# Eight-layer network on two interleaved streams: wait steps folded into instruction steps, and new turn tables

## The chip, the cores and the metric

One NeuronCore of one Trainium2 chip runs the whole program. The metric is device time in microseconds (us) of one execution; several executions are timed and their median is quoted. The profile is of one further execution, taken by the hardware profiler.

## The reference

Four sequences of 512 tokens by 128 features pass through eight residual layers, all in float32. Each is `x = x + layer(layernorm(x))`:

```python
x = x + L0_attn(ln(x))   # 0: state-space scan, 16 heads, conv of width 4, gate, layer norm, projection
x = x + L0_ffn(ln(x))    # 1: token-shift mix, sigmoid gate, squared relu
x = x + L1_attn(ln(x))   # 2: Mamba block, inner width 256, 16 states, softplus, exp, scan
x = x + L1_ffn(ln(x))    # 3: top-2 of 8 experts, gelu
x = x + L2_attn(ln(x))   # 4: causal linear attention, 16 heads
x = x + L2_ffn(ln(x))    # 5: ternary weights, silu, two gelu layers
x = x + L3_attn(ln(x))   # 6: gated selective scan, RMS norm
x = x + L3_ffn(ln(x))    # 7: top-2 of 8 experts, silu gate
```

## The kernel before

The four sequences are played as two streams, here called stream a (sequences 0 and 2) and stream b (1 and 3). A stream runs its layers one after the other for its first sequence, then for its second; layers 3 and 7 (the experts) may take both sequences of a stream at once (`PLAYS`). Stream a takes layers 0 to 6 twice and then layer 7 for both; stream b takes layers 0 to 2 twice, then layer 3 for both, then layers 4 to 6 twice, then layer 7. Below, "b 7" is stream b in layer 7, and a second pass is called so. Each stream has its own four PSUM banks and its own working tiles, so that one stream's work can fill the other's waits.

Every engine runs one instruction list, in which the two streams are interleaved by hand-made tables. On each engine a layer is a Python generator; each `yield` ends a *turn*. `RUNS[engine]` lists run lengths: so many turns of stream a, so many of stream b, and so on. `walk` takes them in that order, so the tables are the instruction order. A turn is no instruction: it holds zero or more waits on semaphores and the instructions behind them. An engine takes its list in order, so a wait of one stream holds back all that stands behind it, of the other stream too. SyncE issues nearly all loads and stores (`SP_MOE`, `SP_ALONE` give the order inside an expert layer); the expert weights go through a ring of 4 slots, and the load of block q waits until block q-4's result has been added (L627, after the DVE instruction of L1421).

Names used later. In layer 2: `m_scan` waits at L1338 and L1340, the scans at L1341, and ScalarE's silu of the convolved rows at L882, the eight-row copy L885, softplus L890 to L895, the decays `exp` L908. In the experts: TensorE up L1829 (layer 3) and L1858 (layer 7 and the down products), ScalarE's gelu L957 and silu L954, DVE's product L1459 and result L1421, the gathers of results by GpSimd L727, and the weighted sum L1432. Layer 5: ScalarE's silu L984. Layer 6: `exp` at L1006 and from L1017 on. SyncE: expert weights L629, slots in L637, results out L641, final output L647.

In some places a wait has a turn to itself, or a turn is empty: in the Mamba layer on TensorE (L1755) and on DVE (L1337), in `turn_block` (L1662), before the scores (L1699), in layers 1 and 5 of TensorE.

## Time and profile before

| | us |
|---|---|
| median of 3 runs | 1415.96 |
| lowest, highest run | 1413.04, 1419.31 |
| span of the profiled execution | 1400.6 |
| TensorE busy | 1104.8 (79%) |
| DVE (VectorE) busy | 890.9 (64%) |
| ScalarE (ACT) busy | 630.4 (45%) |
| GpSimd (POOL) busy | 281.7 (20%) |

The profile gives the time from the first to the last instruction (the span), busy time of each engine, TensorE's granted clock as a share of full speed, the chain of work that ended last, and each instruction with what released it. The median of the timed runs is 15.4 us above the span; the profile's own time beyond its span is not given apart.

### The profile page before, as it was taken

The page shows a single profiled execution, that of the slowest core. Times are in us where ns is not written, and L with a number is a line of the kernel's source. Part 1 is how long each engine was busy: PE and PEld are TensorE (multiplying, and loading weights), DVE is VectorE, ACT ScalarE, POOL GpSimd, SP SyncE. Part 2 cuts the span into 40 slices and gives each one's busy share as a digit, 9 for nine tenths or more (in the row PEclk, how much of TensorE's full clock was granted, in tenths as well). Part 3 has the DMA queues.
Part 4 walks back from the last instruction along what each step waited for, and adds up shares of the span by engine and source line. Part 5 has one row for each costly group of instructions (what it writes and reads, how often), then busy time and mean ns, then how long its engine had stood idle before and what let it go on. Part 6 is the DMA issues. An engine that isn't in the chain of part 4 may idle for free.

```text
span 1400.6 us, 15057 instructions
## 1 busy us (share of the span) xinstructions
PE 1104.8 (79%) x4959; PEld 698.7 (50%) x4959; DVE 890.9 (64%) x1919; ACT 630.4 (45%) x1194; POOL 281.7 (20%) x258
## 2 busy tenths in 40 slices
PE   4978657767977979686768676799999899897791
PEld 2536312334743634353457442574555556787781
DVE  6787879987558767767635789723735652363432
ACT  3433385424552348634237972273252434542330
POOL 3000113324120002130230244202000032014404
PEclk9999877777989999878889897999999999899996
DMA  8100000003520000000125420370000014468782
GB/s 322 47 0 1 0 0 0 0 1 118 163 61 1 0 0 1 0 0 0 45 92 177 131 74 21 96 224 21 1 1 0 1 63 132 157 214 283 260 277 69
DMA packets 49411, 107.02 MB, mean 76 GB/s; under 512 B 4840, under 2 KB 32368, under 8 KB 48688
## 3 DMA queue, kind: packets, MB, share of 16 engines
q1 hardware_dynamic: 44656, 92.74, 20.7%
q0 software_dynamic: 4096, 8.40, 2.0%
q10 hardware_dynamic: 576, 4.87, 0.8%
q8 instruction: 41, 0.67, 0.2%
q14 instruction: 42, 0.34, 0.1%
HBM read 91.24 MB, written 14.75 MB: 76 GB/s over the span
## 4 chain that ended last, share of the span: by engine, by line
PE 41%; DVE 22%; ACT 13%; issue 9%; POOL 7%; DMA 6%; SPq 1%; DVEq 0%; POOLq 0%; ACTq 0%
PE ps L1920 6%; PE ps L1638 5%; DMA expert_ring<-in_e_dram 4%; PE ps L1586 4%; PE ps L1752 4%; DVE up L1341 3%; PE ps L1858 3%; POOL slots_dram L717 3%; ACT big L957 2%; PE ps L1692 2%; PE ps L1829 2%; PE ps L1958 2%; DVE big L1348 2%; POOL up L727 2%; PE ps L1909 1%
## 5 line engine op out<-in xcount | busy, mean ns | idle before, releaser
L1858 PE MATMUL ps<-big,expert_ring 128*128 128x128 f32 x1160 | 158.0, 286 | 33.6 <-DMA expert_ring<-in_e_dram 20.4
L1858 PEld LDWEIGHTS ps<-big,expert_ring 128*128 128x128 f32 x1160 | 145.2, 199 | 48.0 <-DMA expert_ring<-in_e_dram 26.9
L1341 DVE TENSOR_TENSOR_SCAN up<-cv,big 128x512 f32<-128x512 f32 x128 | 152.5, 1230 | 21.5 <-ACT cv L908 17.4
L660 POOL TENSOR_TENSOR rstd<-ve,nhalf 128x4 f32<-128x4 f32 (+1 forms) x41 | 47.2, 1153 | 577.2 <-DVE ve L1119 470.6
L1752 PE MATMUL ps<-big,consts 128*128 128x512 f32 x256 | 154.3, 735 | 2.4 <-DVE big L1348 2.4
L697 POOL TENSOR_TENSOR big<-big,mt 128x512 f32<-128x512 f32 x64 | 85.8, 1344 | 279.1 <-ACT mt L901 152.6
L1920 PE MATMUL ps<-big,weights 128*128 128x512 f32 x256 | 115.4, 597 | 0.0
L1769 PE MATMUL ps<-q,row_pick 96*128 96x512 bf16 x128 | 54.5, 448 | 76.6 <-DVE big L1348 61.4
L1829 PE MATMUL ps<-expert_ring,big 128*128 128x128 f32 x792 | 107.6, 280 | 5.9 <-ACT big L957 3.6
L1829 PEld LDWEIGHTS ps<-expert_ring,big 128*128 128x128 f32 x792 | 98.9, 195 | 15.3 <-ACT big L957 9.8
L1459 DVE SCALAR_TENSOR_TENSOR big<-ps,expert_ring,key 128x128 f32<-128x128 f32 x184 | 51.8, 344 | 79.6 <-PE ps L1858 67.4
L908 ACT ACTIVATE cv<-big,nega 128x512 f32<-128x512 f32 x128 | 87.2, 715 | 14.2 <-DVE up L1341 13.6
L954 ACT ACTIVATE key<-ps,expert_ring 128x128 f32<-128x128 f32 x184 | 52.6, 369 | 88.4 <-PE ps L1858 88.3
L901 ACT ACTIVATE mt<-ps 128x512 f32<-128x512 f32 x64 | 38.2, 598 | 115.4 <-PE ps L1769 110.9
L1586 PE MATMUL ps<-weights,big 128*128 128x128 f32 x608 | 79.3, 288 | 11.0 <-DVE big L1355 5.3
L1752 PEld LDWEIGHTS ps<-big,consts 128*128 128x128 f32 x256 | 59.6, 234 | 54.8 <-issue 45.5
L1586 PEld LDWEIGHTS ps<-weights,big 128*128 128x128 f32 x608 | 75.1, 201 | 21.5 <-DVE big L1355 6.9
L1890 PE MATMUL ps<-qkv_parts,selectors_rounded 128*128 128x512 f32 x192 | 72.2, 490 | 16.4 <-DVE up L1496 12.7
L1348 DVE TENSOR_TENSOR big<-up,ps 128x1024 f32<-128x1024 f32 x64 | 77.6, 1213 | 11.6 <-PE ps L1752 10.7
L717 POOL DMA_INDIRECT slots_dram<-cv,key x64 | 64.0, 1000 | 90.4 <-DVE key L1402 72.5
L1638 PE MATMUL ps<-big,mt 128*128 128x512 f32 x160 | 77.4, 643 | 4.3 <-ACT big L808 4.3
L1769 PEld LDWEIGHTS ps<-q,row_pick 96*128 96x128 bf16 x128 | 13.7, 109 | 127.3 <-DVE big L1348 83.5
(247 smaller groups left out, 1943.4 us busy)
## 6 DMA issues: line engine op xcount, KB each, us to landing
expert_ring<-in_e_dram SPq DMA_DIRECT2D x46, 836.0 KB, 5.3
expert_ring<-in_e_dram SPq DMA_DIRECT2D x53, 578.0 KB, 4.4
big<-slots_dram SPq DMA_DIRECT2D x21, 256.0 KB, 3.5
results_dram<-mt SPq DMA_DIRECT2D x21, 256.0 KB, 5.3
weights<-in_w_dram ACTq DMA_DIRECT2D x1, 3072.0 KB, 15.5
slots_dram<-big SPq DMA_DIRECT2D x2, 1024.0 KB, 10.3
weights<-in_w_dram SPq DMA_DIRECT2D x1, 1600.0 KB, 8.6
x<-in_x_dram SPq DMA_DIRECT2D x4, 256.0 KB, 13.6
```

The lines of the kernel that those rows point to most:

```text
L697: pool.tensor_tensor(BIG2[s][:, 1, :], BIG1[s][:, 3, :], MT[s][:, 0:T], ALU.mult).then_inc(m_d1[s], 1)
L717: pool.indirect_dma_start(xs_d[s % NS], bass.IndirectOffsetOnAxis(ap=posu[:, j:j + 1], axis=0), xh[h][:, c, :], None).then_inc(scattered[s ...
L908: act.activation(CV[s][:, j, :], BIG1[s][:, j, :], ACT.Exp, scale=nega[:, j * NM + n:j * NM + n + 1]).then_inc(m_da[s], 1)
L1341: dve.tensor_tensor_scan(UP[s][:, j, PAD:PAD + T], CV[s][:, j, :], BIG2[s][:, j, :], 0.0, ALU.mult, ALU.add).then_inc(m_scan[s], 1)
L1348: dve.tensor_tensor(BIG2[s][:, 2:4, :], UP[s][:, :, PAD:PAD + T], bank(s, 3).unsqueeze(1).broadcast_to([P, 2, T]), ALU.mult).then_inc(m_sc ...
L1586: last = pe.matmul(bank4(s, k)[:, c, :], lhs(b, c), rhs(b), start=(b == 0), stop=(b == blocks - 1))
L1638: last = pe.matmul(bank(s, c), MT[s][:, m:m + P], BIG2[s][:, k, :], start=(k == 0), stop=(k == c))
L1752: pe.matmul(bank(s, j), ident, BIG2[s][:, 2 + j, :], start=(n == 0), stop=(n == NM - 1))\
L1829: last = pe.matmul(bank4(s, 2 + b % 2)[:, 0, :], HID[s][:, b % 4, k * P:(k + 1) * P], wd[:, k * P:(k + 1) * P], start=(k == 0), stop=(k == 3))
L1858: last = pe.matmul(bank4(s, r if m else b % 2)[:, k, :], ring[:, q % RING, r * T + k * P:r * T + (k + 1) * P], XGT[s][:, b // 4 % 4, b % 4 ...
L1890: last = pe.matmul(bank(s, k), SELR[:, m * P:(m + 1) * P], PARTS[:, part, src, :], start=(part == 0), stop=(part == 1))
L1920: last = pe.matmul(bank(s, j), w(name, (4 * b + j) * P, P), BIG1[s][:, src + b, :], start=(b == 0), stop=(b == 3))
```

## The change

The diff has two parts. In the code, turns that hold only a wait or nothing are dropped, and their wait goes into the turn of the instruction behind it. The lists shorten: TensorE from 1237 to 1121 turns, DVE from 903 to 839; ScalarE keeps 704, GpSimd 239, SyncE 157. All five tables of run lengths are then replaced; the three long ones are left out here.

```diff
     "pool": [
-        1, 1, 1, 1, 1, 1, 1, 1, 1, 1, 2, 2, 4, 1, 2, 1, 2, 1, 2, 1, 2, 1, 2, 1, 2, 2, 1, 2, 8, 8, 9, 3, 1,
-        9, 1, 4, 1, 1, 1, 1, 1, 17, 1, 2, 14, 3, 1, 3, 1, 4, 1, 4, 1, 2, 1, 1, 9, 1, 10, 3, 1, 1, 18, 19,
+        0, 1, 1, 1, 2, 1, 1, 1, 1, 1, 2, 2, 3, 1, 1, 1, 1, 1, 2, 1, 3, 1, 2, 1, 3, 1, 1, 1, 1, 2, 8, 8, 9, 2,
+        1, 9, 1, 5, 2, 2, 1, 15, 1, 4, 13, 1, 1, 3, 1, 1, 1, 3, 1, 5, 1, 3, 1, 1, 9, 1, 10, 3, 1, 1, 18, 19,
         16, 16],
     "sp": [
-        1, 1, 23, 35, 57, 7, 1, 6, 1, 4, 1, 20],
+        2, 1, 22, 35, 56, 1, 1, 3, 1, 7, 1, 5, 1, 21],
 }
...
@@ dve, mamba @@
-                    yield
-                    dve.wait_ge(m_scan[s], m_scan.at(s, 4 * n))
                     for j in range(2):
                         yield
+                        if j == 0:
+                            dve.wait_ge(m_scan[s], m_scan.at(s, 4 * n))
                         dve.wait_ge(m_da[s], m_da.at(s, 2 * n + j))
...
@@ pe, turn_block @@
-                    yield
-                    if j >= 2:
-                        pe.wait_ge(l0_yn[s], l0_yn.at(s, j - 2))
                     for c in range(NC):
                         yield
+                        if c == 0 and j >= 2:
+                            pe.wait_ge(l0_yn[s], l0_yn.at(s, j - 2))
...
@@ pe, state_space and feed_forward @@
                     else:
-                        yield
                         pe.wait_ge(l0_key[s], l0_key.at(s, 0))
...
                 pe.wait_ge(wsem[1], 16)
-                yield
                 pe.wait_ge(f0_mix[s], f0_mix.at(s, 0))
...
@@ pe, mamba @@
-                    yield
-
-                    if n == 0:
-                        pe.wait_ge(m_mix[s], m_mix.at(s, 0))
-                        pe.wait_ge(m_sp[s], m_sp.at(s, 1))
                     for k in range(2):
                         yield
+                        if n == 0 and k == 0:
+                            pe.wait_ge(m_mix[s], m_mix.at(s, 0))
+                            pe.wait_ge(m_sp[s], m_sp.at(s, 1))
...
@@ pe, ternary @@
-                        yield
+                        if j or r:
+                            yield
...
-                    yield
-                    if src == 0:
-                        pe.wait_ge(t_h0[s], t_h0.at(s, 3))
                     for j in range(4):
                         for b in range(4):
                             yield
+                            if src == j == b == 0:
+                                pe.wait_ge(t_h0[s], t_h0.at(s, 3))
```

Laying both tables over the generators gives the order of every engine. Four stretches of it, of ScalarE and at the end of SyncE and DVE (a number behind a name is the block or the step; "up" copies, "z" silu, "s" silu, "dt" softplus, "a" exp, "b", "d8", "gt", "xT", "xs" copies; "h" product, "res" result, "gs" weighted sum):

```
ScalarE, b 3 beside a 2 (second pass)
 before  xT b:act8 up0 up1 z0 z1 s0 b:act9 s1 b:gt5 d8 b:act10 dt0 b:act11 dt1
 after   xT up0 b:act8 up1 z0 z1 s0 s1 b:act9 d8 b:gt5 b:act10 dt0 b:act11 dt1
ScalarE, a 3 beside b 5
 before  b:sa0 act8 act9 b:sa1 act10 act11 b:sa2 act12 act13 b:sa3 act14
 after   b:sa0 b:sa1 act8 act9 act10 act11 act12 b:sa2 b:sa3 act13 act14
ScalarE, a 7 beside b 6 (second pass)
 before  act3 b:ea b:xs0 act4 b:xs1 gt4 act5 b:ex act6
 after   act3 act4 b:ea b:xs0 b:xs1 b:ex gt4 act5 act6
SyncE, a 7 ends and b 7 begins
 before  w22 y4 b:w0 b:w1 b:x0 b:x1 b:x2 b:x3 b:w2 y5 b:w3 b:x4 b:w4 b:w5 b:w6 b:x5 out b:w7 b:y0 b:w8 b:w9 out b:w10
 after   w22 b:w0 y4 b:w1 b:x0 b:x1 y5 b:x2 b:x3 b:w2 b:w3 b:x4 b:w4 b:w5 out b:w6 b:x5 b:w7 b:y0 b:w8 out b:w9 b:w10
DVE, the same place (gs0.0 to gs1.1 are of stream a, h and res of stream b)
 before  h1 res0 h2 res1 gs0.0 h3 res2 h4 gs0.1 res3 h5 gs1.0 res4 h6 res5 gs1.1 h7
 after   h1 res0 gs0.0 h2 res1 h3 gs0.1 res2 h4 res3 h5 res4 gs1.0 gs1.1 h6 res5 h7
```

## Rows read from the trace of the kernel before

**Rows 1.** Page, busy time, share of the span and instructions of each engine.
```profile
PE 1104.8 (79%) x4959; PEld 698.7 (50%) x4959; DVE 890.9 (64%) x1919; ACT 630.4 (45%) x1194; POOL 281.7 (20%) x258
```
**Rows 2.** Cores view: span and mean granted TensorE clock.
```profile
core 0: 1400.6 us, clock 0.886
```
**Rows 3.** Page, chain that ended last, shares of the span.
```profile
PE 41%; DVE 22%; ACT 13%; issue 9%; POOL 7%; DMA 6%; SPq 1%; DVEq 0%; POOLq 0%; ACTq 0%
```
**Rows 4.** Groups by form, ScalarE: line, operation, count, busy us, mean ns, share.
```profile
L908 ACT ACT_TABLE_LOAD x19 | 24.4, 1283 | 0.3
...
L1017 ACT ACT_TABLE_LOAD x1 | 1.3, 1283 | 0.0
```
**Rows 5.** Windows view: stretch, its length, busy us of each engine, clock.
```profile
core 0: us, PE busy (x) PEld busy (x) DVE busy (x) ACT busy (x) POOL busy (x), PEclk, DMA share, GB/s
...
210.00:290.00 80.00, 58.47 (x118) 22.48 (x117) 79.97 (x81) 38.44 (x61) 29.61 (x20) 0.77 0.00 0
...
900.00:975.00 75.00, 69.25 (x361) 46.43 (x360) 23.75 (x66) 40.77 (x89) 11.54 (x12) 1.00 0.47 139
...
1180.00:1240.00 60.00, 52.49 (x352) 46.99 (x351) 26.61 (x94) 31.89 (x78) 2.64 (x2) 0.89 0.44 145
1240.00:1400.00 160.00, 108.27 (x879) 103.58 (x877) 61.31 (x252) 46.06 (x147) 45.79 (x48) 0.88 0.69 227
```
**Rows 6.** Chain in order of time, a scan of layer 2: start, us, what.
```profile
187.70 0.53 issue
```
**Rows 7.** Timeline, stream a in its first Mamba: start, us, instruction.
```profile
200.83 1.28 ACT L908 ACT_TABLE_LOAD   x1
```
**Rows 8.** Timeline, b 3 beside a 2, 758 to 766 us.
```profile
759.55 0.75 DVE L1162 SCALAR_TENSOR_TENSOR cv<-up,params,cv 128x512 f32<-128x512 f32 x1
...
760.79 1.28 ACT L882 ACT_TABLE_LOAD   x1
...
764.52 1.28 ACT L957 ACT_TABLE_LOAD   x1
```
**Rows 9.** Timeline, a 3 beside b 5, 924 to 945 us.
```profile
924.76 0.60 ACT L790 ACTIVATE xT<-ps 128x512 f32<-128x512 f32 x1 [0.18 <-PE ps L1577]
...
926.83 1.14 ACT L957 ACTIVATE big<-ps,expert_ring 128x128 f32<-128x128 f32 x4 [1.47 <-PE ps L1858]
...
927.99 1.28 ACT L984 ACT_TABLE_LOAD   x1
...
929.29 0.69 ACT L984 ACTIVATE cv<-ps,params 128x512 f32<-128x512 f32 x1
...
934.08 1.06 PE L1858 MATMUL ps<-big,expert_ring 128*128 128x128 f32 x8
...
944.47 1.28 ACT L984 ACT_TABLE_LOAD   x1
```
**Rows 10.** Timeline, a 7 beside b 6, 1197 to 1209 us.
```profile
1197.09 1.28 ACT L1017 ACT_TABLE_LOAD   x1
...
1206.53 2.05 PE L1858 MATMUL ps<-big,expert_ring 128*128 128x128 f32 x8 [5.91 <-ACT key L954]
```
**Rows 11.** Timelines of DVE, SyncE and GpSimd where a 7 hands over to b 7.
```profile
1280.71 0.29 DVE L1421 TENSOR_TENSOR mt<-ps,expert_ring 128x128 f32<-128x128 f32 x1 [1.05 <-PE ps L1829]
...
1282.86 2.03 SPq L637 DMA_DIRECT2D big<-slots_dram  x4
...
1286.05 0.43 SPq L641 DMA_DIRECT2D results_dram<-mt  x1
...
1294.59 0.98 POOL L727 DMA_INDIRECT up<-results_dram,key  x1 [16.21 <-DMA results_dram<-mt]
```
**Rows 12.** Timeline of DVE, weighted sums of a 7 among b 7.
```profile
1302.73 1.14 DVE L1432 SCALAR_TENSOR_TENSOR x<-up,key,x 128x128 f32<-128x128 f32 x4 [4.52 <-DMA up<-results_dram,key]
...
1313.77 1.13 DVE L1459 SCALAR_TENSOR_TENSOR big<-ps,expert_ring,key 128x128 f32<-128x128 f32 x4
...
1319.28 1.14 DVE L1432 SCALAR_TENSOR_TENSOR x<-mt,key,x 128x128 f32<-128x128 f32 x4 [4.19 <-DMA mt<-results_dram,key]
```

62 rows, old and new, of the table RUNS are left out of this document.

## The prediction

> **What bounds the kernel now.** I read the page first. No engine is full: TensorE is busy 1104.8 us of 1400.6 and DVE 890.9 [rows 1, 2]. The chain that ended last changes hands all the time: 41% TensorE, 22% DVE, 13% ScalarE, 9% issue, the rest GpSimd and DMA [rows 3]. So what bounds the program is how the two streams' instructions stand among each other, stage by stage, and a new order can act everywhere. The windows view says where it can't: from 210 to 290 us DVE is busy 79.97 us of 80 [rows 5]. That is the first Mamba of both streams, and there an order can only shuffle work. From 900 to 975 us TensorE is busy 69.25 us of 75, so at most 5.75 us are to be had there, and from 1180 to 1240 us 60 - 52.49 = 7.5 us [rows 5]. The last 160 us run on the ring of expert weights, with the DMA engines busy 0.69 of the time [rows 5].
>
> **The merging by itself.** A turn is no instruction; every wait of before is still there. Of the 116 turns dropped on TensorE, 72 were empty (60 in Mamba, 8 in `turn_block`, 4 in layer 5) and 44 held a wait; all 64 dropped on DVE held one. Such a turn costs something only where the old table put turns of the other stream between the wait and its instruction, for then these sit behind the wait. Laying the old tables over the code, I find this with a real wait 5 times: TensorE's wait for the copied `xT` in layer 1 (3 times, with `out`, attention products or a down product behind it), and DVE's wait of L1338/L1340 in a 2 (twice, with a result of L1421 behind it). The price of the first kind lies between nothing and the copy waited for, 0.60 us [rows 9]; three of them 0 to 1.8 us. That of the second kind is the 0.53 us by which a scan starts late after such a wait [rows 6], and the instruction waited for, some 0.7 us; twice, 0 to 2.5 us. I take -1.0 us for all five, bounds -4.3 and 0. The other 103 merged waits have their own instruction directly behind them in the old order, and the merge changes nothing: 0.
>
> **The tables.** I counted, for each instruction of stream a, how many of stream b stand ahead of it. Summed moves: 366 places over 1119 turns on TensorE, 312 over 837 on DVE, 193 over 702 on ScalarE, 26 on GpSimd, 5 on SyncE. No instruction moves by more than 6. The largest common shift is in the first Mamba, where b stands 2.1 places further ahead on DVE, and that is the stretch where DVE is full [rows 5]: I cost it at nothing. If DVE weren't full there, b's head start would delay a by two DVE instructions. So this is a fine re-sorting, and what a trace can price of it is below.
>
> *Table loads of ScalarE.* ScalarE loads a function table when the function kind changes among exp, ln, silu, gelu and sigmoid; copy, relu, abs, square bring no load of their own here. There are 20 groups of such loads, 95 in all, each 1.283 us [rows 4]. Counting kind changes in the old order gives 92 in the tables' part and 3 in the setup: the same 95. The same count in the new order gives 82 + 3 = 85. So ScalarE does 10 x 1.283 = 12.8 us less. Where:
> - First Mamba, b's second silu now directly behind its first: 2 loads, one of them on the chain (at 200.83 us) [rows 7]. But a's `exp` now stands behind b's silu, which waits for b's convolution. I take -0.6, bounds -1.3 and +1.0.
> - b 3 beside a 2: 2 loads of 2.57 us, both on the chain [rows 8]. Again the silu of a's second half must wait for DVE's convolution, which ends at 760.3 us [rows 8], and gelu of block 9 stands behind it and comes later by some 2.7 us, while a's own way to its scans gets shorter. I take the whole -2.6, since the chain runs through a there; bounds -2.6 and +2.7, the latter if the experts of b turn out the later.
> - a 3 beside b 5: 8 loads from 927.99 to 947 us [rows 9] become 4: 5.1 us less. TensorE's idle time there is 5.75 us and most of the rest is product work [rows 5], so some of it won't come through: I take -3.0, bounds -5.1 and 0.
> - a 7 beside b 6: 2 loads less. TensorE waits 5.91 us for ScalarE at 1206.53, which is behind the batch of `exp` that began with a load at 1197.09 [rows 10]. I take -2.6, bounds -5.9 and 0.
>
> The Trainium skill ("ScalarE: Activation LUTs", section "What ACT_TABLE_LOAD costs") gives about 2.66 us for a switch, 1283 ns of load and some 1380 ns of drain. The trace agrees with the load and not with the drain: gelu ends at 926.83 + 1.14 = 927.97, the load starts at 927.99, and silu starts at 929.29 [rows 9]. By the page the loads would be worth 26.6 us instead of 12.8, and the total below would be twice as large in that term; I go by the row.
>
> *The end of a 7.* The last store of results, y5, was ready when DVE ended at 1281.00 us, but SyncE had four slot loads and a weight load queued ahead of it, and these waited for the scatter until 1282.86; y5 went out at 1286.05 and released GpSimd's gathers at 1294.59 [rows 11]. In the new order only two slot loads (about 0.5 us each) are ahead: it goes out at about 1283.9, 2.1 us earlier. The slot loads x2, x3 and w2 behind it go out 0.5 us later. I take -1.5, bounds -2.3 and 0.
>
> *The weighted sums.* They now stand ahead of b's products: gs0.0 ahead of h2, gs1.1 ahead of h6. Both wait for gathers (4.52 and 4.19 us in the trace [rows 12]). h6 ran at 1313.77, while gs1.1 could only start at 1319.28 [rows 12]; with gathers 2.1 us earlier gs1.1 ends at about 1318.3, so h6 comes some 4.5 us later and res5, which frees the slot for w9, with it. Against that res3, res4 and h7 come about 1 us earlier. SyncE's `out` also stands one weight load earlier and waits for the same sums. What is queued behind: all of b's weight loads. I take +1.0, bounds 0 and +4.5.
>
> *Everything else* (some 900 places of small moves) can't be priced from rows one by one: 0, with the clock (below) as its spread.
>
> **Sum.** -1.0 - 0.6 - 2.6 - 3.0 - 2.6 - 1.5 + 1.0 = -10.3 us. Against the profiled execution: 1400.6 - 10.3 = 1390.3 us of span. The runs' median stands 15.4 us above the span and I keep that: 1415.96 - 10.3 = 1405.7, rounded 1405.5 us. The bounds add up to -21.5 (1394.5 us) and +8.2 (1424.2 us).
>
> **Rivals.**
> 1. *The loads were covered.* ScalarE is busy only 45% [rows 1]; where TensorE or the DMAs end last anyway, a shorter ScalarE buys nothing. For it: TensorE's 69.25 of 75 us in the stretch with 4 of the 10 loads [rows 5]. Against it: the loads of a 2 and b 6 are on the chain. Then only -2.6 of the tables, -1.0 and -0.5 at the end remain: about -4, so 1412 us.
> 2. *TensorE's clock falls, and the kernel gets slower.* Grouping silus and gelus makes TensorE's waits rarer but longer. Eight products of 128 columns took 1.06 us in the dense stretch at a granted clock of 1.00 (2.4 GHz) and 2.05 us right after a wait of 5.91 us, the lower level of 1.2 GHz [rows 5, 9, 10]. The mean clock is 0.886 [rows 2], so a loss of 0.01 of it is 0.01 x 1400.6 = 14 us of full-speed work, of which TensorE's 41% of the chain [rows 3] makes 5.7 us, or 6.5 us at the present mean. From a mean of about 0.870 on, the gain of 10.3 is gone; at 0.860 it is +17 - 10 = +7, 1423 us. Every new order throws this die anew; a rise by 0.01 is as possible. The Trainium skill ("TensorE: Matmul & The Clock Gate", Part 1) says that the throttled state is the default and activity releases it. By that rule fewer long waits in 1180 to 1240 us would raise the clock, and longer ones lower it.
> 3. *The new waits at the end bite.* Should every block of b 7 inherit the 4.5 us of h6 and should the gathers' start not move, the end gives +4.5 instead of -0.5, and with half of the loads' gain it is about 1415 us: no change.
> 4. *The change doesn't do what it says*: loads stay at 95, or the moves cancel: 1416 us.
>
> **How the numbers follow.** More than 0.5% (7.1 us) is about what a measurement of this kernel can tell from no change; that puts the borders at 1408.9 and 1423.0. The forecast, with its own range 1396 to 1408.9: 0.52. Rival 1: 0.22; rival 3: 0.08; rival 4: 0.04, all of them inside the borders. Rival 2: 0.14, of which 0.12 is above the upper border and 0.02 within. Faster 0.52, same 0.22 + 0.08 + 0.04 + 0.02 = 0.36, slower 0.12. For the range I take the bounds of the sum and 0.01 of clock downwards in price, -21.5 and some more being unlikely all at once: 1390 to 1421 leaves out about 1 in 10 on either side.
>
> **What would show it.** In the profile after: 85 table loads, four between silu and gelu where a 3 meets b 5, ScalarE busy about 618 us; y5 out within 1.5 us of the slots' arrival; TensorE's wait near b 6's `exp` shorter than 5.91 us; DVE still full in the first Mamba. A mean clock under 0.875 would speak for rival 2, one over 0.895 would give more than I count. The forecast is wrong if ScalarE is busy 12 us less and the span is not shorter (rival 1), or if the gain sits in stretches without a table load, which would mean that the small moves, costed at 0, carried it.

## The result

The kernel after takes 1433.23 us (median of 9 runs, 1425.85 to 1439.34) where the kernel before takes 1419.31 (9 runs beside it, 1413.01 to 1424.77): 1.0113 times as long, 95% interval 1.0089 to 1.0138. Two more sessions gave 1.0088 (1.0058 to 1.0117) and 1.0072 (1.0050 to 1.0095). The forecast was 1405.5 us with a range up to 1421, so it is wrong in its sign, and the measured time is outside the range. The page of after and its cores view (span, mean granted clock), then its windows over the stretches of [rows 5]:

```profile
PE 1104.4 (77%) x4959; PEld 700.5 (49%) x4959; DVE 896.3 (62%) x1919; ACT 614.2 (43%) x1184; POOL 279.6 (19%) x258
PE 47%; DVE 21%; ACT 10%; issue 9%; DMA 7%; POOL 3%; another core or an unknown queue 2%; SPq 1%; DVEq 0%; POOLq 0%; ACTq 0%
core 0: 1437.5 us, clock 0.888
```
```profile
core 0: us, PE busy (x) PEld busy (x) DVE busy (x) ACT busy (x) POOL busy (x), PEclk, DMA share, GB/s
210.00:290.00 80.00, 51.40 (x102) 19.87 (x103) 77.39 (x75) 37.36 (x61) 27.42 (x19) 0.79 0.00 0
900.00:975.00 75.00, 70.17 (x363) 49.73 (x364) 27.46 (x57) 33.86 (x83) 14.63 (x16) 0.97 0.51 151
1180.00:1240.00 60.00, 51.41 (x337) 44.63 (x338) 24.03 (x75) 31.93 (x78) 1.04 (x1) 0.89 0.49 159
1240.00:1400.00 160.00, 120.10 (x925) 114.89 (x924) 61.23 (x261) 47.41 (x151) 33.30 (x34) 0.86 0.68 223
```

ScalarE is busy 614.2 us instead of 630.4 [rows 1] with 10 instructions fewer: the ten saved table loads are there (12.8 us; the other 3.4 us are not accounted for). The clock has not fallen (0.888 against 0.886 [rows 2]). But DVE, busy 79.97 us of the 80 from 210 to 290 us [rows 5], is now busy 77.39, in a stretch in which it can't afford to be idle.

The two profiles alone mislead. Their spans differ by 37 us, the medians by 14. The same semaphore events of both traces, set against each other, stand 8 to 10 us apart from 250 to 400 us, 2 to 6 from 450 to 725, 12 to 14 at 1100 to 1200, and 36 to 38 from 1300 us on. The last jump is not of the change, as the first four experiments show.

### The profile page after: what moved, and what is told of

It reads as the page before. It is cut to its first block, busy times and chain, and to the rows that moved or that the text cites. A ratio compares the mean times of both kernels' runs of the same rounds, so it can differ in the third digit from the quotient of the medians.

```text
span 1437.5 us, 15046 instructions
## 1 busy us (share of the span) xinstructions
PE 1104.4 (77%) x4959; PEld 700.5 (49%) x4959; DVE 896.3 (62%) x1919; ACT 614.2 (43%) x1184; POOL 279.6 (19%) x258
## 4 chain that ended last, share of the span: by engine, by line
PE 47%; DVE 21%; ACT 10%; issue 9%; DMA 7%; POOL 3%; another core or an unknown queue 2%; SPq 1%; DVEq 0%; POOLq 0%; ACTq 0%
PE ps L1917 6%; PE ps L1640 5%; PE ps L1855 5%; DMA expert_ring<-in_e_dram 5%; PE ps L1751 5%; DVE up L1343 3%; PE ps L1588 3%; PE ps L1826 3%; DVE big L1350 2%; PE ps L1887 2%; PE ps L1693 2%; PE ps L1955 2%; PE ps L1875 1%; POOL rstd L662 1%
## 5 line engine op out<-in xcount | busy, mean ns | idle before, releaser
L1855 PE MATMUL ps<-big,expert_ring 128*128 128x128 f32 x1160 | 162.3, 292 | 43.5 <-ACT key L956 21.2
L1855 PEld LDWEIGHTS ps<-big,expert_ring 128*128 128x128 f32 x1160 | 149.8, 204 | 57.5 <-issue 31.1
L1343 DVE TENSOR_TENSOR_SCAN up<-cv,big 128x512 f32<-128x512 f32 x128 | 157.9, 1268 | 19.6 <-ACT cv L910 14.3
L1826 PEld LDWEIGHTS ps<-expert_ring,big 128*128 128x128 f32 x792 | 101.8, 199 | 17.7 <-ACT big L959 8.6
L1350 DVE TENSOR_TENSOR big<-up,ps 128x1024 f32<-128x1024 f32 x64 | 77.9, 1218 | 7.5 <-PE ps L1751 5.5
```

The costliest lines, as they stand in the source:

```text
L1343: dve.tensor_tensor_scan(UP[s][:, j, PAD:PAD + T], CV[s][:, j, :], BIG2[s][:, j, :], 0.0, ALU.mult, ALU.add).then_inc(m_scan[s], 1)
L1350: dve.tensor_tensor(BIG2[s][:, 2:4, :], UP[s][:, :, PAD:PAD + T], bank(s, 3).unsqueeze(1).broadcast_to([P, 2, T]), ALU.mult).then_inc(m_sc ...
L1826: last = pe.matmul(bank4(s, 2 + b % 2)[:, 0, :], HID[s][:, b % 4, k * P:(k + 1) * P], wd[:, k * P:(k + 1) * P], start=(k == 0), stop=(k == 3))
L1855: last = pe.matmul(bank4(s, r if m else b % 2)[:, k, :], ring[:, q % RING, r * T + k * P:r * T + (k + 1) * P], XGT[s][:, b // 4 % 4, b % 4 ...
```

## The experiments

All kernels below are the kernel after with other turn tables, unless said otherwise. A joined order takes on each engine one kernel's order up to the first item of a named stage, and the other kernel's order for all that is left. I call a 0, a 1, b 2, ... the stages as in the prediction. Line numbers in the views are each kernel's own: the scan of layer 2 is L1341 before, L1349 or L1348 in kernels with other tables and L1343 in e7. "Beside" a run stand runs of before in the same session, and "before" in brackets is their median. Stretches: *early* (up to a's first expert layer, about 290 us), *middle* (to a's last expert layer, about 1100 us), *last*.

### Which part of the order costs

**e1**: order of before everywhere, waits merged. The instruction order of each engine is the one of before, line for line.

```diff
     "pool": [
-        0, 1, 1, 1, 2, 1, 1, 1, 1, 1, 2, 2, 3, 1, ...
+        1, 1, 1, 1, 1, 1, 1, 1, 1, 1, 2, 2, 4, 1, ...
```


> The merged turns of the kernel after, with turn tables that give every engine exactly the instruction order of the kernel before; only the places of the waits differ. Theory A (the new order is what costs, the merge costs nothing): within 3 us of before, ratio 0.998 to 1.002. Rival B (the merge itself costs, because a wait that used to be met early on the engine now stands directly ahead of its instruction): about the whole of the 1.1% stays, ratio 1.008 to 1.013. My prediction had the merge alone at -1.0 us (ratio 0.999).

**e2**: before's order early, after's behind it.

```diff
     "dve": [
-        1, 1, 1, 1, 1, 1, 1, 1, 11, 2, 1, 3, 1, 1, 4, ...
+        1, 1, 1, 1, 1, 1, 5, 1, 7, 2, 1, 3, 4, 1, 1, ...
         ... (the last 251 runs as they were)
```


> Order of before on every engine up to the first item of the stream a's first expert layer (about the first 290 us: set-up, the first state-space layer, the first Mamba), order of after behind it, turns merged. Theory A1 (the first Mamba's new order costs the 8 to 10 us by which the same semaphore events of the two profiles stand apart at 200 to 290 us): 7 to 10 us faster than after, ratio to before 1.004 to 1.006. Rival A2 (the shift is given back later or was a matter of that one profile, and the cost arises at the hand-over of the last expert stages): as slow as after, ratio 1.010 to 1.013.

**e3**: after's order early and in the middle, before's in the last part.

```diff
     "dve": [
-        ..., 3, 2, 2, 2, 4, 1, 3, 1, 1, 3, 3, 1, ...
+        ..., 3, 2, 2, 1, 2, 1, 4, 1, 2, 4, 6, 3, ...
```


> Order of after up to the first item of the stream a's last expert layer on each engine (about 1100 us), order of before behind it. Theory A1 (the first Mamba costs 8 to 10 us, the rest little): as slow as after or 1 to 3 us faster, ratio 1.008 to 1.012, and the two long stalls of 14 us around the expert gathers that the profile of after shows are also here. Rival A2 (the hand-over from stream a's to stream b's last expert stage costs what the profiles show between 1250 and 1300 us, 25 us in that one profile and some of it in the median): at least 8 us faster than after, ratio at most 1.005.

**e0**: the kernel after, unchanged.


> The kernel after once more, to see whether the jump of 25 us between 1250 and 1300 us belongs to its order. If it does, the second profile has the two waits of 14 us with nothing known to end them again and a distance of 30 us or more to before's profile; if it was a matter of that one execution, the second profile has a span of 1424 to 1434 us and the distance there is under 10 us. Ratio 1.009 to 1.014 either way.

Measured on one chip (before 1422.92 us there): e1 0.9983 (0.9963 to 1.0003), e2 1.0002 (0.9979 to 1.0026), e3 1.0116 (1.0093 to 1.0138), e0 1.0088 (1.0058 to 1.0117). The merge costs nothing: its interval ends at +0.03%. The early order costs: e2, without it, is 0.86% below e0. (e2 came out faster than either of its two expectations had it.) In the traces of e2 and e3, the same events stand 2.3 us apart at 50 us, 4.5 at 140, 10.9 at 300, and between 9.9 and 10.2 from 400 to 900 us, where both run the same instructions in the same order. The jump at 1300 us is in e1 as well (+20 us against the profile of before), with before's instruction order. So the new order isn't its cause. A later session then gave the other parts, each alone on before's order:

**e14** early, **e12** middle, **e13** last part of after's order.

```diff
# e14, against e1
     "pool": [
-        1, 1, 1, 1, 1, 1, 1, 1, 1, 1, 2, 2, 4, 1, ...
+        0, 1, 1, 1, 2, 1, 1, 1, 1, 1, 2, 2, 3, 1, ...
# e12, against e1
     "act": [
-        ..., 2, 3, 7, 2, 12, 2, 3, 3, 1, 1, 5, 7, ...
+        ..., 2, 3, 7, 1, 2, 1, 7, 1, 2, 1, 4, 3, ...
# e13, against e1
     "dve": [
-        ..., 3, 2, 2, 1, 2, 1, 4, 1, 2, 4, 6, 3, ...
+        ..., 3, 2, 2, 2, 4, 1, 3, 1, 1, 3, 3, 1, ...
```


> Order of after up to the first item of stream a's first expert layer (about 290 us), order of before behind it. Theory (the whole loss is early): at 300 us the events stand 8 to 11 us later than in the profile with the old order, ratio 1.007 to 1.011. Rival (a third of the loss needs the new order of the later stages too): ratio 1.003 to 1.006.

> Order of after only between the first items of stream a's first and last expert layers (about 290 to 1100 us: here stand 6 of the 10 saved table loads, 2 at b 3 beside a 2 and 4 at a 3 beside b 5). My prediction has -5.6 us for it, ratio 0.996. Rival (the loads were covered, the later silu costs elsewhere what it saves): 0 to +5 us, ratio 1.000 to 1.004; together with e2, e3 and the second run of after the medians point to this one.

> Order of after only from the first item of stream a's last expert layer on (about 1100 us: 2 table loads at b 6, the last store y5 ahead of two slot loads, the weighted sums ahead of products). My prediction has -2.6 - 1.5 + 1.0 = -3.1 us, with the merge -4.1, ratio 0.997. Rival (nothing of it comes through, or the weighted sums cost the 4.5 us of their bound): ratio 0.999 to 1.002.

Measured (before 1421.75 us): e14 1.0061 (1.0036 to 1.0086), e12 1.0064 (1.0040 to 1.0088), e13 0.9962 (0.9939 to 0.9985). Against e1's 0.9983 these are +0.78%, +0.81% and -0.21%. From here on such a difference from e1 joins two ratios of two sessions and carries some 0.3% either way: e14 and e12 are clear of zero, e13 isn't. With the merge's -0.17% the parts sum to 1.0121, above the three values of after (1.0113, 1.0088, 1.0072). e14 lies between its two cases: the early loss is not the whole. The middle loses too, where the prediction had -5.6 us and the rival up to +5; e12 is above both. But the runs that hold two parts are lower than their parts: e2, with the middle and the last part, 1.0043 by the sum and 1.0002 measured; e3, with the early part and the middle, 1.0142 and 1.0116. Taken from these the middle costs 0.40% (e2 against e13) or 0.55% (e3 against e14) instead of 0.81%. Its sign is the same three times, its size is known to a factor of two.

### The early part

**e4**: e1 with GpSimd's first two instructions exchanged. **e5**: after's order up to a's first Mamba. **e6**: after's order only from there to a's first expert layer.

```diff
# e4, against e1
     "pool": [
-        1, 1, 1, 1, 1, 1, 1, 1, 1, 1, 2, 2, 4, 1, ...
+        1, 2, 2, 1, 1, 1, 1, 1, 2, 2, 4, 1, ...
# e5, against e1
     "act": [
-        ..., 1, 1, 9, 3, 2, 2, 1, 1, 2, 2, 3, 1, 4, ...
+        ..., 1, 1, 9, 2, 3, 4, 2, 2, 3, 1, 4, 2, 1, ...
# e6, against e1
     "dve": [
-        ..., 2, 1, 1, 2, 2, 2, 1, 1, 3, 1, 2, 1, 6, ...
+        ..., 2, 1, 1, 1, 2, 2, 1, 2, 4, 2, 6, 1, 4, ...
```


> The kernel of e1 (merged turns, order of before) with one exchange: GpSimd's first two instructions, the rstd of stream b ahead of that of stream a, as in the kernel after. Theory (a's first norm waits for b's variance, which comes 1.6 us later, and TensorE has nothing else to do at the start): every event of the layers up to the first Mamba is 2.1 to 2.4 us later than in e1's profile, and the time is 2 to 3 us above e1, ratio to before 0.9995 to 1.001. Rival (what is lost at the start is absorbed when DVE is full from 210 us on): the shift is 0 to 1 us at 300 us and the ratio 0.998.

> Order of after up to the first item of stream a's first Mamba on each engine (start, state-space layer, feed-forward layer of a), order of before from there. Theory (the early loss has three parts: 2.3 us by GpSimd's exchange, 2.1 us around 110 to 140 us where a transposition block of a and DVE's residual add of a stand ahead of work of b that was ready, 6 to 7 us in the Mamba itself): 4.5 us later than e1 in the profile from 150 us on, and 4 to 5 us above e1 in time, ratio 1.001 to 1.002. Rival (DVE's full stretch 210 to 290 us swallows what comes before it): 0 to 1.5 us later from 300 us on, ratio 0.998 to 0.9995.

> Order of before up to the first item of stream a's first Mamba, order of after up to the first item of a's first expert layer, order of before again. Theory (the order within the Mamba costs by itself): from a's first gating product to a's last one 117 to 120 us instead of 111.4, four or five scans of 1.5 to 2.2 us instead of 1.23, all later events 6 to 7 us later than in e1, ratio 1.002 to 1.004. Rival (the loss in the Mamba comes from the two streams' phase at its entry, that is from the earlier changes, and not from its own order): 111 to 113 us there, ratio 0.998 to 0.9995.

Measured (before 1396.29 us, another chip): e4 1.0012 (0.9991 to 1.0033), e5 1.0010 (0.9987 to 1.0034), e6 1.0031 (1.0009 to 1.0053). Against e1: e5 +0.27%, e6 +0.48%, together 0.75%, and e14 has 0.78%. By time only the Mamba's loss is clear of zero; for the start it is the traces that show one.

*The start.* GpSimd computes the first `rstd` of both streams. Its timelines in e1 and e4 (start, duration, instruction, idle time before), and DVE's first norm in each:

```profile
15.60 1.05 POOL L667 TENSOR_TENSOR rstd<-ve,nhalf 128x4 f32<-128x4 f32 x1 [13.06 <-DVE ve L1126]
16.98 1.04 POOL L667 TENSOR_TENSOR rstd<-ve,nhalf 128x4 f32<-128x4 f32 x1 [0.34 <-DVE ve L1126]
...
16.81 2.36 DVE L1140 TENSOR_SCALAR cv<-x,mv,rstd 128x128 f32<-128x128 f32 x8
```
```profile
17.62 2.04 POOL L667 TENSOR_TENSOR rstd<-ve,nhalf 128x4 f32<-128x4 f32 x2 [15.08 <-DVE ve L1126]
...
19.69 2.14 DVE L1140 TENSOR_SCALAR cv<-x,mv,rstd 128x128 f32<-128x128 f32 x8 [2.16 <-POOL rstd L667]
```
With b's `rstd` in front, a's waits for b's variance. DVE's first statistics start at 14.02 us in e1 and at 14.65 in e4, so the norm follows them after 2.79 us in e1 and after 5.04 in e4: +2.2 us. All 12 profiles with before's GpSimd order here have 2.79, all 8 with after's have 5.04. But e6, with the old start and on e4's chip, stands within 0.2 us of e4 from 75 to 150 us, so in these two profiles nothing of it is left. Profiles of one and the same start lie up to 3 us apart there, so one pair doesn't settle whether the 2.1 to 2.4 us last. In time e4 is 0.29% above e1, with overlapping intervals and on another chip: not settled either. What holds over all profiles is the sum of the start. a's first gating product stands at 177.5 to 181.2 us in the 12 profiles with before's start (mean 179.6), and at 181.9 to 185.9 in the 7 with after's (mean 183.2): +3.6 us. Besides the exchange it holds what the expectation of e5 names: the events of e5 are 0.2 to 0.6 us behind those of e4 from 80 to 110 us and 4.9 us from 140 to 200. Which of the moves in between does it isn't shown.

*The Mamba.* From a's first gating product (`big<-cv,up`) to its first closing step (`big<-big,params,ps`) the time is 110.4 to 112.4 us in all 12 profiles with before's order there (mean 111.1) and 117.8 to 118.9 in all 6 with after's (mean 118.4; e7 and e8, below, left out), whatever the start: +7.3 us. Windows over this way in e13 (old) and e6 (new):

```profile
178.41:288.80 110.39, 75.76 (x151) 28.89 (x151) 107.08 (x113) 62.95 (x94) 33.73 (x23) 0.78 0.00 0
```
```profile
181.21:298.99 117.78, 79.53 (x149) 29.87 (x150) 111.26 (x114) 58.21 (x90) 32.50 (x23) 0.77 0.00 0
```
DVE has the same 46 scans in both and is busy 4.2 us longer, with 3.2 us more of idle time (117.78 - 111.26 = 6.52 against 3.31). DVE and GpSimd in e6 show where the busy time comes from:

```profile
227.78 3.41 POOL L705 TENSOR_TENSOR big<-big,mt 128x512 f32<-128x512 f32 x2 [5.80 <-ACT mt L909]
232.66 1.28 POOL L705 TENSOR_TENSOR big<-big,mt 128x512 f32<-128x512 f32 x1 [1.47 <-DVE up L1349]
237.49 2.03 POOL L705 TENSOR_TENSOR big<-big,mt 128x512 f32<-128x512 f32 x1 [3.55 <-DVE up L1349]
```
```profile
228.16 1.97 DVE L1349 TENSOR_TENSOR_SCAN up<-cv,big 128x512 f32<-128x512 f32 x1
...
232.55 1.22 DVE L1356 TENSOR_TENSOR big<-up,ps 128x1024 f32<-128x1024 f32 x1
```
(A line with x2 joins two instructions: the products of the first line start at 227.78 and 229.01.) Most scans take 1.23 us; the one that starts at 228.16, within GpSimd's product, takes 1.97. GpSimd's product of 1.28 us takes 2.03 where it starts behind the start of a scan (237.49). DVE's own L1356, which reads PSUM, keeps its 1.22 us beside a product (232.55 and 232.66 us). How much is lost depends on how much of the first one is left: the six long scans of e6 and of before (1.51 to 2.22 us) all end 1.08 us after the product within which they started, and a product that starts behind a scan's start ends 1.05 to 1.08 us after that scan. So the later of the two runs nearly whole after the earlier. In before's order most of GpSimd's products start beside such PSUM instructions, and 6 of the 23 behind the start of a scan, where the product is the one that takes longer; one of the 46 scans is over 1.45 us. In after's order four or five of the 46 are, and 4 products. The Trainium skill ("SBUF — State Buffer", section "Who interferes with whom") calls the pair of SBUF ports that DVE and GpSimd share an exclusive lock: a DVE instruction with two SBUF inputs contends with a GpSimd instruction that reads SBUF, one with at most one SBUF input, outside the 2-port modes, doesn't. The trace agrees in which instructions collide, and these 1.05 to 1.08 us fit a lock. Two runs take GpSimd's product away almost wholly:

**e7** (order of after) and **e8** (order of before): the products of the Mamba layers are computed for 8 columns only.

```diff
-                    pool.tensor_tensor(BIG2[s][:, 1, :], BIG1[s][:, 3, :], MT[s][:, 0:T], ALU.mult).then_inc(m_d1[s], 1)
+                    pool.tensor_tensor(BIG2[s][:, 1, 0:8], BIG1[s][:, 3, 0:8], MT[s][:, 0:8], ALU.mult).then_inc(m_d1[s], 1)
```


> The kernel after with GpSimd's products of the Mamba layers (the second half of the decay's input, 128x512) cut to 8 columns: that part of the computation is left out, the rest is as it was. Theory (in the first Mamba of after, GpSimd's products fall on DVE's scans, and both take longer: five scans stand at 1.5 to 2.2 us): every scan up to 300 us is at 1.22 to 1.25 us, and the way from a's first gating product to its last takes 113 to 115.5 us instead of 118.8. Rival (the long scans have another cause, such as the operand still being written or the wait for ScalarE, and GpSimd's product only happens to lie beside them): the same scans stay at 1.5 to 2.2 us and the way is 117 us or more.

> The control to the run with GpSimd's products of the Mamba layers cut to 8 columns (that part of the computation is left out), here with the order of before. Theory (in the old order only one of 46 scans falls on such a product): the way from a's first gating product to its last, 110.4 to 112.4 us in five runs, gets shorter by 0 to 2 us only, to 109.5 to 111.5, against 6.1 us for the new order. Rival (the products slow down either order alike): it falls by 5 us or more.

The same way in e7 and e8:

```profile
183.05:295.69 112.64, 75.34 (x147) 27.95 (x148) 106.80 (x114) 58.25 (x90) 5.99 (x23) 0.80 0.00 0
```
```profile
177.91:286.56 108.65, 75.08 (x151) 28.96 (x151) 104.46 (x113) 63.91 (x95) 9.72 (x24) 0.81 0.00 0
```
No scan is above 1.45 us in either. Each was profiled once, they ran on different chips, and only this way is compared. It falls by 5.8 us in after's order (118.4 to 112.6), by 2.4 in before's (111.1 to 108.65, 0.9 us beyond what I had expected), and the distance between the orders from 7.3 to 4.0 us. So about 3 us of the 7.3 are the collisions; with one profile each and 2.0 us between equal profiles the figure is rough. A rival is that the shorter product only ends waits for its result; but in e6 DVE waits for it once on this way, for 0.6 us.

The other 4.0 remain without collisions. DVE is idle 5.84 us against 4.19 on this way and busy 2.3 us longer, though the durations of its instructions add up to nearly the same, 112.4 us in e7 and 112.0 in e8. What differs is how they follow each other. e7, then e8:

```profile
231.66 1.22 DVE L1343 TENSOR_TENSOR_SCAN up<-cv,big 128x512 f32<-128x512 f32 x1
232.92 1.22 DVE L1350 TENSOR_TENSOR big<-up,ps 128x1024 f32<-128x1024 f32 x1
234.06 0.68 DVE L1335 TENSOR_TENSOR big<-ps,big 128x512 f32<-128x512 f32 x1
234.77 1.22 DVE L1343 TENSOR_TENSOR_SCAN up<-cv,big 128x512 f32<-128x512 f32 x1
```
```profile
230.23 0.68 DVE L1340 TENSOR_TENSOR big<-ps,big 128x512 f32<-128x512 f32 x1
230.83 1.21 DVE L1355 TENSOR_TENSOR big<-up,ps 128x1024 f32<-128x1024 f32 x1
231.96 2.33 DVE L1348 TENSOR_TENSOR_SCAN up<-cv,big 128x512 f32<-128x512 f32 x2
```
In e8 each instruction starts 0.08 us before the one ahead of it ends. In e7 the product of L1350 stands right behind the scan that it reads, and the scan right behind the product of L1335 that it reads, and each starts 0.03 us after the other's end. In after's order the closing product stands directly behind a scan 18 times on this way and a scan behind that product 18 times, in before's 8 and 7 times; 36 instructions start so late instead of 17 (35 to 37 against 16 or 17 in all profiles). Nineteen times 0.11 us are 2.1 us of the 4.0; 0.4 us more are longer instructions and 1.0 us longer waits. In before's order an instruction of the other stream mostly stands between the two. This is read from the traces; no run changes it alone.

### The middle part

**e15**, **e16**, **e17**: after's order only from a's first expert layer to a's second Mamba (290 to 700 us), to a's second expert layer (to 870 us), to its last (to 1100 us), one stretch each.

```diff
# e15, against e1
     "pool": [
-        ..., 8, 8, 9, 3, 1, 9, 1, 4, 1, 1, 1, 1, 1, 17, 1, 2, 14, ...
+        ..., 8, 8, 9, 2, 1, 9, 1, 5, 2, 2, 1, 15, 1, 4, 14, 3, 1, ...
# e16, against e1
     "act": [
-        ..., 1, 2, 5, 1, 1, 5, 1, 1, 1, 1, 1, 1, 1, 7, ...
+        ..., 1, 2, 5, 2, 1, 5, 1, 1, 2, 1, 1, 5, 2, 5, ...
# e17, against e1
     "act": [
-        ..., 1, 21, 6, 1, 1, 1, 5, 11, 1, 1, 1, 2, 1, 2, ...
+        ..., 1, 21, 6, 2, 5, 1, 1, 8, 1, 3, 2, 5, 2, 2, ...
```


> Order of after only from the first item of a's first expert layer to the first item of a's second Mamba (about 290 to 700 us; no saved table load there). From the profiles: b's second Mamba takes 128.9 us instead of 131.2 to 133.5 from its first gating product to its last, so -2.3 us, ratio 0.9965. My prediction had 0 for it, with the merge 0.998. Rival (the loss of the middle part is here, in small moves around the state-space layer beside expert layers): 1.001 or more.

> Order of after only from the first item of a's second Mamba to the first item of a's second expert layer (about 700 to 870 us; two saved table loads, each 1.28 us). Theory (b's grouped silu makes a's second gating wait, as my upper bound had it): from a's convolution to its first gating product 20.9 us instead of 20.1, from there to its last 96.7 instead of 95.5, so +2.0 us and ratio 0.9995 to 1.001. My prediction had -2.6 us, ratio 0.996.

> Order of after only from the first item of a's second expert layer to the first item of its last one (about 870 to 1100 us; four saved table loads). Theory (the loads lay beside TensorE's work and gave nothing, and the way between the first gating products of b's and a's factored layers, 63.7 to 65.4 us in the old order, takes 66.4 to 68.1 us): +2 us in the profile, ratio 1.000 to 1.002. My prediction had -3.0 us, ratio 0.996. If nearly the whole 0.8% of the middle part is here (ratio above 1.004), the loss is at the hand-over that this order sets up, and not in the stretch.

Measured (before 1397.08 us): e15 0.9990 (0.9968 to 1.0012), e16 1.0034 (1.0013 to 1.0055), e17 1.0028 (1.0004 to 1.0051). Against e1 these are +0.07%, +0.51% and +0.45%, in sum 1.03% where e12 has 0.81%. e15 isn't clear of zero (expected were -2.3 us and 0.9965); e16 and e17 are, if barely in e17, and both are above their expectations.

*e16, b 3 beside a 2.* Against the profile of before its events go from -4.6 us at 725 to +2.8 us at 875: it loses 7.4 us. Two profiles with the old order in this stretch drift the same way, e15 by 1.0 and e1 by 2.7 us. In time e16 loses 7.1 us (0.51% of 1397) with some 4 us either way. It has 93 table loads instead of 95. ScalarE in e15, with the old order in this stretch, and in e16:

```profile
780.40 0.60 ACT L909 ACTIVATE mt<-ps 128x512 f32<-128x512 f32 x1 [1.55 <-PE ps L1772]
...
785.98 0.62 ACT L909 ACTIVATE mt<-ps 128x512 f32<-128x512 f32 x1
...
790.18 0.58 ACT L909 ACTIVATE mt<-ps 128x512 f32<-128x512 f32 x1
```
```profile
785.94 0.60 ACT L909 ACTIVATE mt<-ps 128x512 f32<-128x512 f32 x1 [2.57 <-PE ps L1772]
...
791.68 0.60 ACT L909 ACTIVATE mt<-ps 128x512 f32<-128x512 f32 x1 [1.35 <-PE ps L1772]
792.58 1.14 ACT L965 ACTIVATE big<-ps,expert_ring 128x128 f32<-128x128 f32 x4 [0.30 <-PE ps L1861]
...
797.41 0.60 ACT L909 ACTIVATE mt<-ps 128x512 f32<-128x512 f32 x1 [1.04 <-PE ps L1772]
```
In the old order ScalarE comes late to two of these three results of TensorE and doesn't wait. In the new one it waits for TensorE each time. The windows from 775 to 800 us, e15 first, then e16, and the two largest groups of ScalarE's waits from 740 to 800 us (us in total, times, longest):

```profile
775.00:800.00 25.00, 22.81 (x117) 15.94 (x118) 19.98 (x24) 22.59 (x44) 6.12 (x5) 0.89 0.38 106
```
```profile
775.00:800.00 25.00, 18.36 (x87) 12.48 (x86) 18.07 (x22) 19.58 (x36) 6.36 (x5) 0.79 0.23 72
```
```profile
ACT big L965 <- PE ps L1861: 3.0, 2, 1.9
ACT mt L909 <- PE ps L1772: 2.3, 2, 1.5
```
```profile
ACT mt L909 <- PE ps L1772: 5.7, 4, 2.6
ACT big L965 <- PE ps L1861: 5.2, 4, 2.3
```
5.3 us of waits in the old order, 10.9 in the new, against 2.6 us of loads saved. The same clock times hold somewhat different work in the two runs. Taken by the same ScalarE instructions, to the end of the stretch, e15 first, then e16:

```profile
736.80:863.70 126.90, 93.91 (x421) 56.92 (x419) 98.35 (x159) 85.49 (x161) 41.37 (x35) 0.83 0.34 100
```
```profile
737.70:869.90 132.20, 91.54 (x421) 57.17 (x419) 98.41 (x160) 83.19 (x160) 41.49 (x35) 0.89 0.33 97
```
ScalarE has 2.3 us less to do and takes 5.3 us longer. This work takes 126.3 to 130.8 us in the 11 profiles with the old order here (mean 127.6) and 130.3 to 133.5 in the 7 with the new (mean 131.3): +3.7 us, with ScalarE's idle time up from 42.0 to 48.1. The clock isn't the cause: TensorE's granted clock is lower in the new order from 775 to 800 us (0.79 against 0.89), but over the whole work it is higher (0.89 against 0.83).

*e17, a 3 beside b 5.* The windows from 920 to 960 us in e15 (old there) and e17:

```profile
920.00:960.00 40.00, 37.06 (x187) 24.46 (x186) 6.94 (x18) 24.73 (x49) 7.35 (x8) 1.00 0.49 137
```
```profile
920.00:960.00 40.00, 38.31 (x195) 25.82 (x194) 6.88 (x18) 19.88 (x47) 7.66 (x8) 1.00 0.48 140
```
ScalarE has 4.85 us less to do. TensorE had 2.9 us of free time left in the old order, so hardly more could come through, and in these 40 us it is busy 1.25 us more. Four loads are gone (91 in all). From the ScalarE instruction at 863 us to the one at 960 the way is 95.7 us in the mean of the 11 profiles with the old order and of the 7 with the new: the loads gave nothing. Behind it, from 960 to 1120 us, the new order takes 163.6 us instead of 161.8 in the mean, with ranges that overlap (159.6 to 165.8 and 159.6 to 163.9). In e17's time the loss is 0.45%, 6.3 us with some 4 either way; what of it goes beyond the 1.8 us I can't place. Its expectation was +2 us.

### The last part and the chips

**e18**: after's order from a 3 to a's second Mamba and in the last part, before's elsewhere. **e19** (the kernel after) and **e20** (e18 again) were run side by side in one more session.

```diff
# e18 and e20, against e1: the edits of e15 and e13 together
     "dve": [
-        ..., 2, 1, 1, 1, 1, 1, 3, 1, 1, 2, 22, 1, 4, ...
+        ..., 2, 1, 1, 2, 3, 1, 2, 1, 1, 1, 19, 1, 1, ...
```


> Order of after in two parts only: from a's first expert layer to its second Mamba, and from a's last expert layer on; order of before elsewhere, turns merged. If parts add up as the profiles show them (-2.3 us and, measured, -0.2% for the last part beside the merge's -0.17%), the ratio is 0.993 to 0.996, better than either kernel. Rival (parts don't add, the last part's gain hangs on the phase in which the streams enter it): 0.997 to 1.001.

> The kernel after, once more, beside the joined order. If the chip is the faster kind (before near 1396 us): the last part's new order gains 8 us there instead of 3, so after is slower by only 0.3% to 0.8%, ratio 1.003 to 1.008, and its way from the last factored layer to the end is 205 to 209 us. If it is the slower kind (before near 1420 us): 1.009 to 1.013 as before, and 232 to 239 us.

> The joined order (before's, with the order of after from a's first expert layer to its second Mamba and from a's last expert layer on; turns merged), once more beside after. On the faster kind of chip 0.993 to 0.997 again. On the slower kind the parts measured there (merge 0.9983, last part -0.21%, and -0.1% for b's second Mamba) give 0.994 to 0.998. A rival, that the gain of 0.9953 was that chip's alone: 0.999 to 1.001 on the slower kind.

Measured: e18 0.9953 (0.9934 to 0.9972) where before takes 1397.08 us; e20 0.9978 (0.9955 to 1.0001) and e19 1.0072 (1.0050 to 1.0095) where before takes 1419.66. So the joined order beats both kernels, by 0.5% on the one chip; on the other it beats after by 0.9%, and before by 0.2%, whose interval still holds no difference. After in e19 is a little better than the 1.009 to 1.013 expected for that kind of chip.

GpSimd's first scatter of b 7 (a scatter or gather is 16 indirect transfers), in e15 and in e18:

```profile
1253.42 1.03 POOL L725 DMA_INDIRECT slots_dram<-cv,key  x1 [20.76 <-DVE key L1410]
```
```profile
1240.82 1.03 POOL L725 DMA_INDIRECT slots_dram<-cv,key  x1 [14.57 <-DVE key L1410]
```
DVE's routing turns of b 7 (two of logits, one of ranks) stand ahead of results of a 7 in the new order, and the scatter, with slot loads and gathers behind it, comes 12.6 us earlier, 1.4 of them because e18 enters the last factored layer so much earlier. y5 goes out behind two slot loads instead of four, and the first gather starts at 1277.2 us instead of 1289.0. From the last factored layer's gating (`big<-cv,up`, at 1168 to 1199 us) to the end e18 takes 206.6 us, e15 213.0.

The profiles fall into two groups there. In the sessions with before at 1396 to 1397 us this last way is 213.0 to 217.3 us in the old order (6 profiles), 205.6 (e7, which leaves out GpSimd's products) and 206.6 in the new; in the sessions with before at 1419 to 1423 us it is 236.6 to 239.5 (5 profiles) and 231.2 to 238.9 (6). The first profile of before has 216.3. Windows from 1262 to 1345 us of before and of e1, whose instruction order is the same:

```profile
1262.00:1345.00 83.00, 63.37 (x491) 60.55 (x490) 29.76 (x112) 26.25 (x86) 27.72 (x29) 0.92 0.84 283
```
```profile
1262.00:1345.00 83.00, 47.57 (x329) 45.00 (x329) 22.12 (x82) 17.70 (x57) 27.60 (x29) 0.77 0.61 198
```
The chain of waits of after names it:

```profile
1273.00 14.45 another core or an unknown queue
1323.03 14.41 another core or an unknown queue
```
Both begin in the stretches of 20 us in which GpSimd issues its 16 indirect transfers; in e1 the core's transfers move 198 GB/s in that window instead of 283. All 11 profiles of the slower group have one to three such waits of 6 to 19 us on their chain there, those of the faster group none. The kind goes with the session, whatever the kernel: four sessions were slow and two fast, and the five whose chip is recorded all ran on different ones. Whether it is the chip or the hour, and what the cause is, is not shown; below I say chip.

## Why the prediction was wrong

**The merge** (-1.0 us, bounds -4.3 and 0): e1 has -0.17%, 2.4 us, interval -5.3 to +0.4. Within its bounds.

**The table loads, their number** (85, ScalarE busy about 618 us): right in the number, 85; ScalarE is busy 614.2 us.

**First Mamba, -0.6 us, and its moves at nothing**: this step failed first. Of the stretch "where DVE is full" the prediction says "I cost it at nothing". A full engine shows that nothing can be gained; it shows nothing of what can be lost. The busy time is itself made by the order, for it depends on what GpSimd does beside each scan and on what stands between an instruction and the one that reads its result. The new order cost 7.3 us on this way (6.7 in time): about 3 by the collisions, some 2 by instructions right behind their inputs, the rest by waits. The upper bound I gave for the whole stretch was +1.0 us. The rows of before had both halves of the collisions, 79.97 us of DVE and 29.61 us of GpSimd in [rows 5]; I never laid them over each other.

**The start**, not named in the sum: +3.6 us at 180 us. "26 places on GpSimd" were costed at 0 together; the first of them puts the first norm 5.04 us behind the first statistics instead of 2.79, though that alone didn't last in the one pair of profiles on one chip. Most of the rest arises between 110 and 140 us, by moves that no run singles out.

**b 3 beside a 2, -2.6 us, bounds -2.6 and +2.7**: measured +7.1 in time, with some 4 us either way, and +3.7 in the traces of this stretch. I had named the mechanism (what stands behind the grouped silu comes later) and sized it by one block of the experts. The saved 2.3 us of ScalarE's work came back as 6 us of idle time. That this is a lead over TensorE which ScalarE lost is my reading of the waits; no run isolates it.

**a 3 beside b 5, -3.0 us, bounds -5.1 and 0**: the loads were covered, as rival 1 had it; measured +6.3 in time, of which the traces place about 2, behind the loads and not beside them.

**The last part, -2.6 - 1.5 + 1.0 = -3.1 us**: e13 against e1 gives -0.21%, 3.0 us, which isn't clear of zero; e18 against e15, in one session, -0.37%, 5.2 us. The sign is right and the size fits, but partly by luck, for the reason is only half of it. y5 did go out ahead of two slot loads, but what moved the gathers was the scatter, 12.6 us earlier, by turns of routing that I had costed at 0.

**The step from span to time** (+15.4 us) was false as well. In the runs of after, time and span of one run lie about 2 us apart. The other 13 fit the distance between two chips, for by its last way (216.3 us) the profiled execution of before was on the faster kind, and its timed runs were on the slower. It didn't change the forecast's difference, only gave the 1400.6 us a false meaning.

**Rivals.** Rival 2 gave a slower kernel by a falling clock: 0.888 against 0.886 in the profiles, and in e0's session 0.888 to 0.896 in the five runs of after against 0.875 to 0.892 in the 24 of before. The clock didn't fall, and the kernel got slower all the same. Rival 1 was true where TensorE was full. That the small moves could cost 0.8% in each of two parts was no rival of mine, though I had written that they "can't be priced": 900 places without a price were given 0 and no width of their own.

## What to carry to other kernels

"This engine is full, so an order can't matter there" bounds the gain only. Look in such a stretch at what each neighbour does beside each of the full engine's instructions, and at how often one of these stands right behind the one whose result it reads, and give a re-ordering there a loss of some per cent of the stretch (here 7.3 of 111 us) as its bound. A saved instruction on an engine that runs behind another's results is worth something only if the engine keeps its lead. And a table of turns can be taken apart: joining the parts of two orders that pay gave 0.5% less than before on one chip and 0.2% less, not clear of noise, on another, where the whole change gives 0.7% more. Only a part whose gain is clear of noise should be carried over: of the changes here that is the last one.

## What the runs showed of the hardware

- A DVE scan of 128x512 takes 1.23 us. One that starts within GpSimd's product of two SBUF operands ends 1.08 us after that product, so it takes up to 2.2 us; the product (1.28 us) that starts behind a scan's start ends 1.05 to 1.08 us after it. A DVE product with a PSUM operand keeps its 1.22 us.
- In the first Mamba a DVE instruction that needs not wait starts 0.08 us before the end of the one ahead of it, and 0.03 us after that end where it reads that one's result: 0.11 us each time (17 times on the way through the first Mamba in before's order, 36 in after's).
- The same kernel runs at 1396 us in the sessions on two chips and at 1420 us in those on others. 22 us of the difference lie in the last 240 us, where the slower ones have one to three waits of 6 to 19 us on their chain that begin while GpSimd issues indirect transfers.
- The same order enters the first Mamba at 177.5 to 181.2 us in 12 profiles: a single pair of profiles can't tell 3 us.
